# Scoring stage of an attention layer on one core: one operand of each two-operand DVE pass held in PSUM

## What is computed

```
proj_s = feature @ W_s.T
proj_t = feature @ W_t.T
z = proj_s[src] + proj_t[dst]
z = jnp.where(z >= 0, z, NEG_SLOPE * z)      # NEG_SLOPE = 0.2
e = (z @ W_attn.T)[:, 0]
m = jax.ops.segment_max(e, src, num_segments=n)
e_exp = jnp.exp(e - m[src])
denom = jax.ops.segment_sum(e_exp, src, num_segments=n)
alpha = e_exp / denom[src]
agg = jax.ops.segment_sum(feature[src] * alpha[:, None], dst, num_segments=n)
return agg @ W_fc.T + b_fc
```

## Time and profile before

| | |
|---|---|
| time, median of 3 runs | 8335.23 us (8322.83 to 8339.7) |
| the profiled execution's own time | 8342.56 us |
| its span in the trace | 8340.9 us |
| mean granted PE clock | 0.866 of full speed |
| busy: PE, DVE, POOL, ACT | 5871.6, 5253.5, 4872.2, 3108.6 us |

### The profile page before, as it was taken

The page is one execution under the profiler, slowest core; times in us unless marked ns, Lnnn a source line. Parts: engine busy times, 40 slices in busy tenths (PEclk is TensorE's granted clock), DMA queues, the critical chain, the costliest instruction groups (busy, mean ns, idle before and its releaser), DMA issues. The chain is left out here.

```text
span 8340.9 us, 150068 instructions
## 1 busy us (share of the span) xinstructions
PE 5871.6 (70%) x21918; PEld 3629.9 (44%) x21919; DVE 5253.5 (63%) x17536; ACT 3108.6 (37%) x9803; POOL 4872.2 (58%) x6011
## 2 busy tenths in 40 slices
PE   5997999046779997677999777776656779300476
PEld 3771344035544444554444444444225558200355
DVE  5999888044569995455666555655854569433764
ACT  2990455004655552364444211111113557200156
POOL 1557777747522224764777677776567633676342
PEclk8995899569989998899999888888888989655799
DMA  3660000027966665797888755554016977421167
GB/s 90 211 208 15 1 1 1 1 87 250 307 227 246 243 247 177 221 310 264 319 319 310 243 189 185 191 190 161 1 51 209 302 250 230 109 54 43 56 207 229
DMA packets 801335, 1450.36 MB, mean 174 GB/s; under 512 B 136831, under 2 KB 543383, under 8 KB 801236
## 3 DMA queue, kind: packets, MB, share of 16 engines
q1 hardware_dynamic: 236788, 752.87, 26.3%
q10 hardware_dynamic: 413792, 410.91, 15.5%
q0 software_dynamic: 150656, 285.54, 12.2%
HBM read 803.24 MB, written 645.70 MB: 174 GB/s over the span
## 5 line engine op out<-in xcount | busy, mean ns | idle before, releaser
L1134 PE MATMUL merge_banks<-merge_rows,merge_mask 128*128 x6264 | 1630.4, 416 | 711.3 <-SPq L1103 420.5
L1134 PEld LDWEIGHTS merge_banks<-merge_rows,merge_mask 128*128 128x128 f32 x6264 | 1249.9, 206 | 1091.8 <-issue 908.5
L1116 DVE TENSOR_SCALAR merge_mask<-ramp,dst_at,soft_at_step 128x128 f32<-128x128 f32 x2349 | 848.2, 366 | 985.8 <-PE merge_banks L1134 862.0
L1228 POOL DMA_INDIRECT merge_rows<-h,merge_take_i x1176 | 1130.3, 961 | 565.0 <-issue 292.0
L1770 PE MATMUL node_p_out<-w,node_h_t 128*128 128x259 f32 (+2 forms) x4704 | 1437.8, 428 | 26.0 <-ACT node_h_t L1809 24.0
L1166 ACT COPY merge_total<-merge_banks 128x256 f32<-128x256 f32 x1568 | 577.6, 369 | 1169.6 <-PE merge_banks L1134 1047.4
L1683 POOL TENSOR_TENSOR node_inv_std<-node_var,node_minus_half 128x4 f32<-128x4 f32 x392 | 467.2, 1192 | 859.8 <-DVE node_var L1620 540.0
L1770 PEld LDWEIGHTS node_p_out<-w,node_h_t 128*128 128x128 f32 x4704 | 744.9, 190 | 286.2 <-issue 219.5
L1748 PE MATMUL node_p_turn<-ident,node_xn 128*128 128x128 f32 x3136 | 619.3, 279 | 176.9 <-DVE node_xn L1577 87.8
L1770 PE MATMUL node_p_out<-w,node_kept_t 128*128 128x512 f32 x1568 | 740.9, 595 | 0.0
L1748 PEld LDWEIGHTS node_p_turn<-ident,node_xn 128*128 128x128 f32 x3136 | 405.7, 141 | 719.0 <-issue 441.8
(11 more groups left out here) (435 smaller groups left out, 10801.0 us busy)
## 6 DMA issues: line engine op xcount, KB each, us to landing
merge_held<-own ACTq DMA_DIRECT2D x196, 512.0 KB, 5.7
x<-merge_total ACTq DMA_DIRECT2D x196, 512.0 KB
node_x<-x SPq DMA_DIRECT2D x196, 512.0 KB, 5.6
node_x<-in_x SPq DMA_DIRECT2D x194, 512.0 KB
h<-node_rows_h SPq DMA_DIRECT2D x98, 512.0 KB, 4.1
merge_held<-h ACTq DMA_DIRECT2D x98, 512.0 KB
mix<-merge_total ACTq DMA_DIRECT2D x98, 512.0 KB
node_mixed<-mix SPq DMA_DIRECT2D x98, 512.0 KB, 4.3
```

The source lines that it names most:

```text
L1116: ins = nc.vector.tensor_scalar(mask[j][:], k.ramp[:, 0:P], columns(k.dst_at, s), columns(weight, s), ALU.is_equal, ALU.mult)
L1134: nc.tensor.matmul(banks[:, bass.ds(nc.s_assert_within(at[2 * j + 1], 0, (BANKS - 1) * 512, skip_runtime_bounds_check_because=small), D)], ...
L1228: nc.gpsimd.indirect_dma_start(rows[:, (j + n) * D:(j + n + 1) * D], None, table, bass.IndirectOffsetOnAxis(take_i[:, j + n:j + n + 1], 0) ...
```

## The change

DVE gets one operand of each of its three two-operand passes from PSUM, and ACT puts them there.

- Once, ahead of the tiles, `attn` is copied to PSUM (`p_attn`).
- For each tile ACT copies the gathered row `a[j]` to PSUM (`p_a`, two buffers) and, once DVE's add is done, writes 0.2 z to PSUM (`p_low`, two buffers).
- The add reads `p_a` and `b[j]`; the bend is a plain max of `p_low` and z into the new `bent_z`; the product sum reads `bent_z` and `p_attn`.
- DVE's order is another: in tile t it adds t, places t-3 (both one-hots now stand in `place`), and bends and scores t-2. ACT copies row t, scales t-1 and keeps product t-4.
- The products have two PSUM buffers instead of four.

```diff
-    p_h = [ph.ps(f"p_h{n}", [P, 512]) for n in range(G)]
+    p_h = [ph.ps(f"p_h{n}", [P, 512]) for n in range(2)]
+    p_a = [ph.ps(f"p_a{n}", [P, 512]) for n in range(2)]
+    p_low = [ph.ps(f"p_low{n}", [P, 512]) for n in range(2)]
+    p_attn = ph.ps("p_attn", [P, 512])
...
             def place(t, j, first):

                 dve.wait_ge(scored, t + 1)
                 if not (first and j < HOT):
                     dve.wait_ge(placed, t - HOT + 1)
+                nc.vector.tensor_scalar(at_low[j % HOT][:], k.ramp[:, 0:P], columns(low, t), None, ALU.is_equal
+                                        ).then_inc(low_hot, 1)
                 nc.vector.tensor_scalar(at_high[j % HOT][:], k.ramp[:, 0:NT], columns(high, t), score[:, j:j + 1],
                                         ALU.is_equal, ALU.mult).then_inc(high_hot, 1)
+
+            def bend(t, j, first):
+
+                dve.wait_ge(lowered, t + 1)
+                if not (first and j < 2):
+                    dve.wait_ge(scored, t - 1)
+                nc.vector.tensor_tensor(bent_z[j % 2][:], p_low[j % 2][:, 0:D], z[j % 4][:], ALU.max).then_inc(bent, 1)
+                dve.wait_ge(bent, t + 1)
+                if not first:
+                    dve.wait_ge(high_hot, t - 3)
+                nc.vector.tensor_tensor_reduce(junk[:], bent_z[j % 2][:], p_attn[:, 0:D], 1.0, 0.0, ALU.mult, ALU.add,
+                                               score[:, j:j + 1]).then_inc(scored, 1)

             def tiles(i, first, n):
...
+                    dve.wait_ge(a_in, t + 1)
+                    if not (first and j < 4):
+                        dve.wait_ge(bent, t - 3)
+                        dve.wait_ge(lowered, t - 3)
+                    nc.vector.tensor_tensor(z[j % 4][:], p_a[j % 2][:, 0:D], b[j][:], ALU.add).then_inc(added, 1)
+                    if not (first and j < 3):
+                        place(t - 3, (j - 3) % R, first)
                     if not (first and j < 2):
+                        bend(t - 2, (j - 2) % R, first)
...
-                    if not (first and side == 0):
-                        pe.wait_ge(h_made, t - G + 1)
+                    if not (first and j < 2):
+                        pe.wait_ge(h_made, t - 1)
...
+            BEHIND = 4
...
+                    if j % LAG == 0:
+                        act.wait_ge(got[j // LAG], 16 * 2 * LAG * (i + 1))
+                    if not (first and j < 2):
+                        act.wait_ge(added, t - 1)
+                    nc.scalar.copy(p_a[j % 2][:, 0:D], a[j][:]).then_inc(a_in, 1)
+                    if not (first and j == 0):
+                        lower(t - 1, (j - 1) % R, first)
+                    if j >= BEHIND:
+                        keep_product(t - BEHIND, j - BEHIND, None if first else i)
```

More of the change, by code:

```diff
@@ L1879, in score_sources @@
     z = [ph.sb(f"z{n}", [P, D]) for n in range(4)]
+    bent_z = [ph.sb(f"bent_z{n}", [P, D]) for n in range(2)]
     junk = ph.sb("junk", [P, D])
@@ L1953, in tiles @@
                     t = i * R + j
-                    z0, z1 = z[2 * (j % 2)], z[2 * (j % 2) + 1]
                     if j % LAG == 0:
                         dve.wait_ge(got[j // LAG], 16 * 2 * LAG * (i + 1))
-                    if not (first and j < 2):
[L1958 to L1974, removed]
+                    dve.wait_ge(a_in, t + 1)
[5 more added lines that the diff above has]
+                        place(t - 3, (j - 3) % R, first)
+                    if not (first and j < 2):
+                        bend(t - 2, (j - 2) % R, first)
             in_tiles(dve, tiles)
+            for t in (NT - 2, NT - 1):
+                place(t - 1, (t - 1) % R, False)
+                bend(t, t % R, False)
             place(NT - 1, (NT - 1) % R, False)
@@ L2001, in _, with keep_product, lower, early @@
         def _(act):
+            BEHIND = 4
+            def keep_product(t, j, uses):
+                side, g = j // G, j % G
+                if g == 0 and uses is not None:
+                    act.wait_ge(h_put[side], 16 * uses)
+                act.wait_ge(product, t + 1)
+                nc.scalar.copy(h[side][:, g, :], p_h[j % 2][:, 0:D]).then_inc(h_made, 1)
+            def lower(t, j, first):
+                act.wait_ge(added, t + 1)
+                if not (first and j < 2):
+                    act.wait_ge(bent, t - 1)
+                nc.scalar.mul(p_low[j % 2][:, 0:D], z[j % 4][:], 0.2).then_inc(lowered, 1)
             def tiles(i, first, n):
                 for j in range(n):
[L2004 to L2008, removed]
+                    t = i * R + j
+                    if j % LAG == 0:
+                        act.wait_ge(got[j // LAG], 16 * 2 * LAG * (i + 1))
+                    if not (first and j < 2):
+                        act.wait_ge(added, t - 1)
[4 more added lines that the diff above has]
+                        keep_product(t - BEHIND, j - BEHIND, None if first else i)
+                    elif not first:
+                        keep_product(t - BEHIND, j - BEHIND + R, early(i))
+            def early(i):
+                return i - 1 if not isinstance(i, int) or i > 1 else None
             in_tiles(act, tiles)
+            lower(NT - 1, (NT - 1) % R, False)
+            for t in range(NT - BEHIND, NT):
+                keep_product(t, t % R, t // R)
         @block.sync
```

4 lines of the change are left out of this document (3 added, 1 removed).

## The result

The changed kernel takes **8266.9 us** (median of 5 runs, 8258.9 to 8285.9) where the kernel before, run beside it, takes 8336.4 (median of 5, 8322.8 to 8345.1). The ratio is 0.992, with a 95% interval of 0.9905 to 0.9938: faster by 0.8%. The forecast was 8264.

A forecast was written before the change was run, and what follows sets the result against it. POOL's gathers were taken to pace the scoring stage. 8342.6 (profiled execution) - 75.7 (shorter gathers) + 4 (stage's end) = 8270.9, and 7.3 less for the median gives 8264 us; own range 8250 to 8283, 8 in 10 within 8246 to 8322.

The forecast's parts named there:

- POOL paces the stage: Scoring stage: POOL waits for nobody, 832.2 us in gathers of 1088; other engines hidden if under 11.1 us a round.
- The gathers' new duration: POOL's 784 gathers in the scoring stage: from 1061.5 to 965 ns each, 75.7 us off.
- DVE's time: DVE in the scoring stage: 1.61 to about 1.8 us a tile, hidden by POOL; 78 us without that cover.
- ACT: ACT in the scoring stage: two more passes per tile, 1.13 us a tile in all, 4.5 us a round, hidden.
- The ring through ACT: PE, ACT and DVE waiting on each other: some 3.6 us for two tiles, nothing lost at 2.4 GHz.
- Rival 3: Scoring stage: PE's ring becomes the bound with the clock at 1.2 GHz; 8443 us by the median, chance 0.10.
- The end of the stage: After the last gather: PE has seven tiles left instead of four; +4 us, ends +2 and +8.
- Why the gathers were long: Scoring stage: DVE's passes with two SBUF operands hold POOL's gathers, 1061 ns against 965 under tensor_scalar alone.
- Rival 2: Scoring stage: the one-hots, not the two-operand passes, hold POOL; gathers stay at 1061 ns, 8339 us, chance 0.10.
- Rival 1: Scoring stage: gathers beginning inside at_high may still wait; 995 ns, 52 us off, +4, so 8287 us, chance 0.15.

The follow-up runs named there:

- attn_ramp_psum: The kernel before with the attention row and the one-hots' ramp held in PSUM, old order kept; 8261.6 us, ratio 0.9911.
- all_sbuf: The changed kernel with all three DVE passes reading SBUF operands again, ACT's copies made but unread; 9812.1 us, ratio 1.019 to the kernel before, on the slower chip.

## Why the prediction was right, and where not

- *POOL paces the stage*: right. The idle time before the gathers is "issue" in both traces, and every kernel of the table follows its gathers: 784 x (1061.5 - 960.1) ns = 79.5 us, and the stage is 80.2 us shorter.
- *The gathers' new duration*, 965 ns from the stage with the same mix: 958.4 and 960.1 measured, 81 us off where 75.7 was forecast. Of the 5 us some 1.6 are the rounding up from that stage's 963.
- *DVE's time*, 1.61 to about 1.8 us, hidden: 1.59 and 1.81 in the two kernels with one gather a tile. The forecast of 78 us without cover came to 86 in the stage. The profile also showed at_low at 313 ns in the mean instead of 287, which I hadn't counted; hidden too.
- *ACT*, 1.13 us a tile: 388 + 380 + 371 = 1.14. Hidden.
- *The ring through ACT costs nothing at 2.4 GHz*: right where the kernel before takes 8336 us, with a mean clock of 0.89. Rival 3, the slower one, didn't come. On the slower chip, where PE's results reach the others late, the new order was dear, and in the way that the prediction describes: "if the product is late, both the next copy to PSUM and DVE's next add stand behind it". It had looked for a late product at a low PE clock only.
- *The end of the stage*, +4: 3.8.
- *Why the gathers were long*: **half wrong**. "Long gathers stand where DVE reads two SBUF operands" holds, but it is not the whole and not the larger part. I gave the order of the passes no share at all, and with ACT's copies, but without any new operand, it gives 35 us. The step that failed is the reading of the earlier trace rows: the gather's end at 5212.70, "when the bend has given way", is a coincidence, as the 61 gathers show that are held as long with no bend behind them. What counts is when it is let in, 0.95 us before its end, and that is the end of the product sum. And the earlier trace rows, taken as a witness, is a weak one: in the nine other traces of this study from chips of this speed, that same stage's gathers take 1012 to 1132 ns with nothing changed in it (1013 and 1026 in the change's two), so 1063 was in part where they happened to fall.
- *Rival 2, the one-hots*: wrong as the whole cause (8339), right as a part. With the ramp in PSUM the gathers that start in at_high fall from 1237 to 952 ns, and the time falls by 39 us. The Trainium skill, "SBUF — State Buffer", section "Who interferes with whom", says that tensor_scalar in a 2-port mode locks GpSimd out, and on that the trace agrees. It also says, as an inference, that a two-SBUF tensor_tensor leaves descriptor generation alone, and there the trace disagrees: a gather that starts in the add takes 1074 ns with two SBUF operands and 952 with one.
- *Rival 1*, that part of the delay stays under at_high: it does, 1005 ns for those that start in it. But they are 109 of 784, 6.6 us in all, where the rival asked for 24 us.

So the time came out by a comparison with a stage of the same mix, which holds whatever the cause is. That the number came out right with the mechanism half wrong is luck. The cause as it was told would have sent a reader to move three operands where one was nearly enough.

## What to carry to other kernels

When POOL's instructions are longer beside a busy DVE, don't stop at which kind of pass stands there: subtract the undisturbed duration from the end, see which pass had just ended when POOL got in, and count this over the stage. Two passes back to back that both read only SBUF can hold POOL through both (here at_high with the product sum behind it did so 172 times of 191, with the bend behind it 8 of 94, and no pair that began with another pass), and an equal period of the two engines repeats it tile after tile. The cheapest cure here is to hold one constant operand of the second pass in PSUM (here 65 of 87 us, for one copy); an order or a ring through a third engine should be weighed against it, the more so as it costs time where one engine's results come late.

## What the hardware showed that I had not expected

The lock works both ways. A one-hot that reads SBUF is sometimes held by a gather; one that reads PSUM is slower, but never held. Duration in ns, least, median, most, of at_low after:

```profile
L1954 DVE TENSOR_SCALAR score_at_low<-ramp,score_low x392: 275/278/523, 4726.2 to 5735.9; 128x128 f32<-128x128 f32 x196
```

and of both one-hots in `attn_ramp_psum`:

```profile
L1966 DVE TENSOR_SCALAR score_at_low<-score_p_ramp,score_low x392: 332/342/347, 4720.6 to 5727.4; 128x128 f32<-128x128 f32 x196
```

```profile
L1952 DVE TENSOR_SCALAR score_at_high<-score_p_ramp,score_high,score_score x392: 668/676/685, 4722.6 to 5729.0; 128x392 f32<-128x392 f32 x196
```

From SBUF at_low's median is 278 ns and its longest 523; from PSUM 342 and 347. The starts and durations of the change's trace show when a gather holds it: all 88 at_low that start between 0.47 and 0.70 us after a gather's start end as if they had begun 0.72 us after it (0.715 to 0.726), and of the others none takes more than 349 ns. at_high takes 676 ns from PSUM against a mean of 491 from SBUF, so `attn_ramp_psum` pays for its shorter gathers with DVE's time: its adds stand 1.86 us apart in the median, against 1.61 before and 1.83 in the change, and this too is hidden only as long as POOL leads.

And chips differ by more than any version here: 9636 us on one against 8332 and 8337 on two others for the same kernel. On the slower one POOL's gathers are no longer than elsewhere (about 990 ns in `all_sbuf`) and land as soon; what comes late there is what the others wait for from PE.
